# Two attention layers with expert layers between: token numbers in tile order, earlier splitting of h, and expert weights split three experts ahead

## The reference

```python
x = x + xattn0(layernorm(x), ctx)     # queries, keys and values from x, 1024 context rows per batch, plus 512 new ones
x = x + ffn0(layernorm(x))            # 8 experts, top 2, inner width 256: silu(x wi0) * (x wi1) wo
x = x + xattn1(layernorm(x), ctx)     # readout of the 1024 masked context rows, no projections
x = x + ffn1(layernorm(x))            # 32 experts, top 8, inner width 192
# x: (2, 512, 512) float32, so 1024 tokens = 8 tiles of 128
```

## Time and profile before

| | us |
|---|---|
| median of 3 runs | 1081.93 (1081.78 to 1082.22) |
| profiled execution, its own time | 1074.04 |
| its span | 1072.3 |
| TensorE busy in the span | 800.4 (75%) |
| GpSimd, ScalarE, VectorE busy | 476.3, 517.8, 517.3 |

### The profile page before, as it was taken

The page is one execution under the profiler, slowest core; times in us unless marked ns, Lnnn a source line. Parts: engine busy times, 40 slices in busy tenths (PEclk is TensorE's granted clock), DMA queues, the critical chain, the costliest instruction groups (busy, mean ns, idle before and its releaser), DMA issues.

```text
span 1072.3 us, 20533 instructions
## 1 busy us (share of the span) xinstructions
PE 800.4 (75%) x5262; PEld 438.2 (41%) x5263; DVE 517.3 (48%) x1531; ACT 517.8 (48%) x764; POOL 476.3 (44%) x397
## 2 busy tenths in 40 slices
PE   3999999999538995477984177777777778777770
PEld 2555455555324442233542043444444444444440
DVE  6344345555444552556884244544544535453432
ACT  2334234445436663135563065566656556655550
POOL 3420000001235774300777555666766566656560
PEclk9999999999769998697996599999999999999995
DMA  8501100000147876901111358878997878779668
GB/s 278 177 20 60 60 31 22 29 31 31 31 130 206 210 174 104 321 2 50 47 47 33 94 134 217 217 156 203 220 233 195 227 168 197 182 186 230 150 111 255
DMA packets 106088, 146.55 MB, mean 137 GB/s; under 512 B 18080, under 2 KB 59296, under 8 KB 106048
## 3 DMA queue, kind: packets, MB, share of 16 engines
q0 software_dynamic: 25760, 56.56, 26.6%
q1 hardware_dynamic: 77696, 89.30, 25.6%
q10 hardware_dynamic: 2592, 0.19, 0.2%
HBM read 103.15 MB, written 42.86 MB: 136 GB/s over the span
## 4 chain that ended last, share of the span: by engine, by line
PE 38%; DMA 18%; issue 11%; DVE 11%; DVEq 8%; ACT 5%; SPq 4%; POOL 3%; ACTq 2%; POOLq 0%
PE pst L181 31%; DMA big<-in_L_ffn_w_down_dram 8%; DMA x_rows<-mid,small 6%; DVEq L1100 3%; DMA mid<-moe_normalised_rows,small 3%; DVEq L1094 2%; PE pst L1204 2%; PE pst L453 2%; POOL moe_tokens_of_experts L934 2%; DMA big<-x_rows 1%; DVE big L1086 1%; DVE xn L284 1%; ACT big L1068 1%; DVE stats L272 1%; PE pst L893 1%
## 5 line engine op out<-in xcount | busy, mean ns | idle before, releaser
L181 PE MATMUL pst<-big,mid 128*128 (+1 forms) x1392 | 278.1, 351 | 28.7 <-DVE mid L1315 16.6
L934 POOL DMA_INDIRECT moe_tokens_of_experts<-token_no,small x80 | 83.7, 1046 | 307.0 <-DVE small L987 286.9
L1398 POOL DMA_INDIRECT x_rows<-mid,small x100 | 161.1, 1611 | 130.2 <-ACT mid L1259 66.4
L181 PEld LDWEIGHTS pst<-big,mid 128*128 128x128 f16 x1392 | 134.6, 100 | 137.7 <-issue 43.8
L1388 POOL DMA_INDIRECT mid<-moe_normalised_rows,small x106 | 113.9, 1075 | 90.3 <-DVE small L1305 29.3
L1204 PE MATMUL pst<-big,mid 128*128 x520 | 129.8, 382 | 1.4 <-ACT mid L1251 0.9
L1240 ACT ACTIVATE mid<-pst 128x1024 f16<-128x1024 f16 x102 | 103.8, 1017 | 54.2 <-PE pst L1176 47.2
L1176 PE MATMUL pst<-id,mid 128*128 128x128 f16 x816 | 64.8, 224 | 59.6 <-DMA mid<-moe_normalised_rows,small 54.2
L1315 DVE SCALAR_TENSOR_TENSOR mid<-pst,small,mid 128x192 f32<-128x192 f32 (+1 forms) x100 | 42.6, 426 | 118.4 <-ACT mid L1246 117.6
L181 PE MATMUL pst<-ctxN,mid 128*128 128x512 f16 x384 | 89.8, 392 | 3.2 <-ACT mid L577 3.2
L1176 PEld LDWEIGHTS pst<-id,mid 128*128 128x128 f16 x816 | 51.6, 100 | 94.4 <-DMA mid<-moe_normalised_rows,small 40.4
(11 more groups left out here) (197 smaller groups left out, 1163.0 us busy)
## 6 DMA issues: line engine op xcount, KB each, us to landing
big<-in_L_ffn_w_gate_dram SPq DMA_DIRECT2D x32, 384.0 KB
big<-in_L_ffn_w_up_dram SPq DMA_DIRECT2D x32, 384.0 KB
big<-in_L_ffn_wi_dram SPq DMA_DIRECT2D x16, 512.0 KB
big<-in_L_ffn_w_down_dram SPq DMA_DIRECT2D x32, 256.0 KB
big<-in_L_ffn_w_down_dram SPq DMA_DIRECT2D x64, 128.0 KB
moe_normalised_rows<-xn SPq DMA_DIRECT2D x18, 256.0 KB, 2.0
mid<-in_ctx_dram SPq DMA_DIRECT2D x16, 256.0 KB, 5.1
x_rows<-big SPq DMA_DIRECT2D x16, 256.0 KB, 8.0
```

The lines of the kernel that those rows point to most:

```text
L181: last = nc.tensor.matmul(dst, stationary(a, c), moving(b, c), start=(k == 0), stop=(k == 3 * len(parts) - 1))
L934: nc.gpsimd.indirect_dma_start(out=self.tab_d[:, :], out_offset=bass.IndirectOffsetOnAxis(ap=self.addr[j % 2][:, k:k + 1], axis=0), in_=to ...
L1398: nc.gpsimd.indirect_dma_start(out=acc_d[p][:, :], out_offset=bass.IndirectOffsetOnAxis(ap=self.si[p], axis=0), in_=self.y[p], in_offset=N ...
```

## The change

- **Token table.** The table in DRAM is laid out expert by expert and tile by tile, 128 numbers per row, so that the numbers of one tile of an expert are one row. SyncE's load of the table is gone. Instead `dve_route` works out the row `tidx` of each tile, GpSimd gathers those rows with one indirect DMA (`table_rows`), and `dve_rows` turns them with one TensorE transpose into `rows`, in which column t+2 holds the numbers of tile t. No column has to be loaded into a register.
- **VectorE's pair.** h of tile t is made and split at once, then come the row numbers for gather t+4 and the weights of t+2, then a split, then the row numbers for scatter t-1. Registers: 2 experts (`etab`) and 3 of `stab`.
- **Splits of weights.** `stab` holds the expert plus 3. ScalarE, GpSimd and VectorE all split expert e+3 in the slot after e's first tile, all in the same slot. `ftab` and its wait are gone.
- **Second expert layer.** Experts 0 to 3 are split within attn1 (ScalarE after iterations 1 to 4; all low halves on GpSimd, two experts before the first listing, one after each of the first two listings). Experts 4 and 5 are loaded meanwhile. In exp0 experts 2 and 3 are split in slots 0 and 1 whatever the tiles are.
- **Order in attention.** `logits` is issued between the two halves of `values`, `choose` and `place` move, GpSimd stores the spare accumulator rows after the first listing, not at the end. Routing semaphores are shared by both layers.

```diff
@@ three / values: the values product in two halves
-        def three(pe, dst, parts, stationary, moving):
+        def three(pe, dst, parts, stationary, moving, first=True, final=True):
...
+                three(pe, dst, range(half), lambda h, k: pT[:, h, k, :], val, final=False)
+                between()
+                three(pe, dst, range(half, n), lambda h, k: pT[:, h, k, :], val, first=False).then_inc(self.pv_full, 1)
@@ Attention.pe
-                    self.values(pe, i)
-                    if self.first and i >= 2:
-                        self.next.logits(pe, i - 2)
-                    if not self.first and i >= 1:
-                        self.next.logits(pe, i - 1)
+                    def between():
+                        if self.first and i >= 2:
+                            self.next.logits(pe, i - 2)
+                        if self.first and i == NT - 1:
+                            self.next.norm_turn(pe, NT - 2, self.norm_bank(NT - 2))
+                        if not self.first and i >= 1:
+                            self.next.logits(pe, i - 1)
+                    self.values(pe, i, between)
@@ Attention.act
+                    if not self.first and 1 <= i <= 4:
+                        self.next.split_early_hi(act, i - 1)
@@ Attention.dve, end of an iteration, and the tail
+                    if i >= (2 if self.first else 1):
+                        self.next.choose(dve, i - (2 if self.first else 1))
...
                 self.update(dve, NT - 1)
                 self.next.norm_row(dve, NT - 1)
-                self.next.choose(dve, NT - 2)
-                self.next.norm_low(dve, NT - 1)
                 self.next.weight(dve, NT - 3)
                 self.next.place(dve, NT - 2)
+                self.next.norm_low(dve, NT - 1)
+                self.next.choose(dve, NT - 1)
+                self.next.place(dve, NT - 1)
                 self.next.weight(dve, NT - 2)
-                self.next.choose(dve, NT - 1)
                 self.next.weight(dve, NT - 1)
-                self.next.place(dve, NT - 1)
@@ Experts
+            AHEAD = 3
...
+                    if not self.late and j in (1, 2, 4, 5):
+                        e = {1: 2, 2: 3, 4: 4, 5: 5}[j]
+                        self.load_next(sp, e, e % 2)
...
-            def table_sp(self, sp):
...
+            def table_rows(self, pool):
+                pool.wait_ge(self.tab_s, 3)
+                for q in range(2):
+                    pool.wait_ge(self.listed[q], 16 * NT // 2 * self.K)
+                nc.gpsimd.indirect_dma_start(out=self.trow, out_offset=None, in_=self.tiles_d[:, :],
+                                             in_offset=bass.IndirectOffsetOnAxis(ap=self.tidx, axis=0)).then_inc(self.trow_in, 16)
...
+            def split_early_hi(self, act, e):
+                if e == 0:
+                    act.wait_ge(back_s, NT)
+                self.split_hi(act, e)
+
+            def split_early_lo(self, pool, e):
+                pool.wait_ge(self.w_hi, 2 * e + 2)
+                nc.gpsimd.tensor_tensor(self.gu[:, e, 1, :, :], self.gur[:, e % 2, :, :], self.gu[:, e, 0, :, :], ALU.subtract).then_inc(self.wgu_lo, 1)
+                nc.gpsimd.tensor_tensor(self.d[:, e, 1, :, :], self.dr[:, e % 2, :, :], self.d[:, e, 0, :, :], ALU.subtract).then_inc(self.wd_lo, 1)
...
+            def dve_rows(self, dve):
+                NE = self.NE
+                dve.wait_ge(self.trow_in, 16)
+                nc.vector.tensor_copy(self.trow32, self.trow).then_inc(self.rows32_s, 1)
+                dve.wait_ge(self.route_pe, 4)
+                link(dve, nc.vector.tensor_copy(self.rows, bank(4)[:, 256:256 + NE]))
@@ act_pair
-                    if not first:
+                    if first:
+                        if self.late:
+                            self.split_hi(act, 2 + p)
+                    else:
                         self.weigh(act, it - 1, t - 2, p)
-                    with act.If(e[p + 1] > e[p]):
-                        self.split_hi(act, e[p + 1], self.first_tile(act, e[p + 1]))
+                        with act.If(e[p + 1] > e[p]):
+                            self.split_hi(act, e[p + 1])
@@ dve_pair
-                e = self.experts(dve, it, 0, 3)
-                c = self.columns(dve, it, -2, 7)
+                e = self.experts(dve, it, 2, 2)
+                x = None if first else self.splits(dve, it)
                 for p in range(2):
                     t = 2 * it + p
-                    self.rows_in_turn(dve, it + 1 + p, t + 3, 1 - p, c[5 + p])
-                    self.weights_in_turn(dve, it + 1 + p, t + 1, 1 - p, e[1 + p])
+                    self.make_h(dve, t, p)
+                    self.h_high(dve, t, p)
+                    self.h_low(dve, t, p)
+                    self.rows_in_turn(dve, it + 2, t + 4, p)
+                    self.weights_in_turn(dve, it + 2, t + 2, p, e[p])
+                    if first:
+                        if self.late:
+                            self.split_d_lo(dve, 2 + p)
+                    else:
+                        with dve.If(x[p + 1] > x[p]):
+                            self.split_d_lo(dve, x[p + 1])
                     if not (first and p == 0):
-                        self.h_high(dve, t - 1, 1 - p)
-                        self.h_low(dve, t - 1, 1 - p)
-                    with dve.If(e[p + 1] > e[p]):
-                        self.split_d_lo(dve, e[p + 1])
-                    self.make_h(dve, t, p)
-                    if not first:
-                        self.rows_out(dve, it - 1, t - 2, p, c[p])
+                        self.rows_out(dve, it - 1 + p, t - 1, 1 - p)
@@ pool_pair
-                e = self.experts(pool, it, 1, 3)
+                e = None if first else self.splits(pool, it)
                 for p in range(2):
                     t = 2 * it + p
                     self.gather(pool, t + 3, 1 - p)
-                    with pool.If(e[p + 1] > e[p]):
-                        self.split_gu_lo(pool, e[p + 1])
-                    if not first:
+                    if first:
+                        if self.late:
+                            self.split_gu_lo(pool, 2 + p)
+                    else:
+                        with pool.If(e[p + 1] > e[p]):
+                            self.split_gu_lo(pool, e[p + 1])
                         self.scatter(pool, it - 1, t - 2, p)
@@ GpSimd's program
+            exp1.split_early_lo(pool, 0)
+            exp1.split_early_lo(pool, 1)
             for j in range(NT):
                 exp1.list_tokens(pool, j)
-            pool.wait_ge(attn1.x_s, NT)
+                if j < 2:
+                    exp1.split_early_lo(pool, 2 + j)
+                if j == 0:
+                    exp1.spare_rows(pool)
             exp1.pool(pool)
```

383 lines of the change are left out of this document (194 added, 189 removed).

## The result

The changed kernel takes **1178.11 us** (median of 4 runs, 1172.60 to 1184.53) where the kernel before takes 1082.08 us (1081.78 to 1087.98): the ratio is 1.087, with a 95% interval of 1.083 to 1.091. It is 8.7% slower. The forecast said slower, but with 1100 us, a range of 1086 to 1116 us, and 1132 us for the dearest rival.

What follows compares the result with a forecast made beforehand. It took VectorE's late low half of h as today's wait and the three-slot gather chain as the next bound. Terms -1 (exp1), +4 (exp0), +15 (early splits), 0 made +18: 1074.0 to 1092, plus 7.9 for the median: 1100 us, range 1086 to 1116.

Steps and rivals of the forecast that it cites:

- a listing block of 8 takes 10.7 us: In attn1, GpSimd lists a block of 8 in 10.7 us, an iteration takes 12, so its queue has little room.
- each before the listing needs its addresses: In attn1, VectorE is held at place(4) to place(7), yet in time for the listing; attn1's own end isn't the bound.
- exp1, "-1 us": Second expert stage: 421 us against 422, from 72 slots at 5.36 us and 8 at 4.40, between 352 and 447.
- This part gives what the gather leaves: down to 4.40 us a slot: Splitting h at once in exp1's loop: three slots at least 13.2 us, one 4.40, 0.88 below today's, 70 us in 80 tiles.
- 2.7 us late: In exp1's loop, splits in one slot send the next gather 6.3 us after the down product's end instead of 3.6.
- exp0, "+4": First expert stage: 4 us gained, splits in the loop cost 7, two unconditional splits 1: +4 us, from -9 to +10.
- Early splits, "+15": Weight splits in attn1 delay the last listing by 15 us, 10 to 18: 8.5 + 10.9 + 1.2 - 5.6.
- "0 us" from the last listing to the first gather: Between attn1's last listing and exp1's first gather: 8.4 to 9.7 us against 8.6 before, so no change.
- The marks: In exp1: last listing near 615, first product 631, scatter 3.7 us behind y's copy, low-half waits under 10, gathers above 60.
- Splits fall into slack: Rival, chance 0.27: the loop's split delays cost little, exp1 374 us instead of 422, exp0 -5, listing +15: 1044 us.
- The scatter's buffer binds: Rival, chance 0.15: scatters landing before y may be rewritten set the slot; exp1 447 us, exp0 +8, listing +15: 1130 us.
- The listing's delay does not show: Rival, chance 0.08: attn1's early splits do not delay the path, since casts come sooner or blocks shrink: +3, 1085 us.

Runs made afterwards that it cites:

- e1: Kernel before, with token numbers written to side-by-side words as in the change and the table read back word by word: ratio 1.084.
- e17: Changed kernel, unchanged, profiled in the same series as the unchanged kernel before: span 1158.4 us, one run.
- e18: Changed kernel with exp1's token numbers 32 bytes apart and low halves subtracted a slot after the cast, early splits kept: 1069.96 us, ratio 1.000 in the medians.
- e4: Changed kernel with GpSimd and VectorE subtracting low halves one slot after ScalarE's cast in both expert loops: 1110.58 us, ratio 1.017.
- e2: Changed kernel with the second expert stage's token numbers 32 bytes apart in memory instead of 4: 1152.27 us, ratio 1.061.
- e13: Changed kernel with low halves a slot after the cast, exp1's weights loaded and split late, and its token numbers 32 bytes apart: 1078.03 us, ratio 0.992.
- e7: e4 with VectorE's copy of the scatter's row numbers one tile later: ratio 1.101.
- e8: Changed kernel with GpSimd issuing the scatter before the low-half subtraction, cast and subtraction still in one slot: 1118.98 us, ratio 1.030.
- e5: Kernel before, with both halves of h made right behind make_h in h's own slot: ratio 1.053.
- e14: e10 plus four pairs of unused GpSimd subtractions in attn1 at the early splits' places, without casts or loads: ratio 1.019.
- e10: Changed kernel with the scatter ahead of the subtraction, exp1's weights loaded and split late, and its token numbers 32 bytes apart: 1079.8 us, ratio 1.008.
- e16: Kernel before, unchanged, profiled again in the same series as the unchanged changed kernel: span 1066.8 us, one run.
- e9: Kernel before, with GpSimd issuing a slot's scatter ahead of the low-half subtraction: ratio 1.030.
- e12: Kernel before, with 32 semaphore increments nobody waits for at the start of ScalarE's, TensorE's and VectorE's programs: ratio 1.000.
- e11: e10 with the low halves also subtracted a slot after the cast: ratio 1.021.

## Why the prediction was wrong

The sign was right. On one chip the change costs 91.6 us where the sum has 18. Of the 73.6 us between them 31 lie in the middle, where a cause of 12 to 32 us was missing, and 32 in exp1, where the gain was put at 70 us and is 22; exp0 has 6 and the start 4.

**The missing cause.** The step that failed is "a listing block of 8 takes 10.7 us", with the half-sentence on VectorE at place(4) to place(7), "each before the listing needs its addresses". The forecast looked at the new addresses only for what the table load costs, and took the landing "as before". The words side by side hold the packets of queue q1, SyncE's, which brings weights and stores rows (78 to 204 ns in e1), and listings land after 5.6 us instead of 2.2 (e1, exp0). Shown by e1, by e17 against e18 (+31.6 us) and by e4 against e2 (+12.1 us). The start of exp0 (+4.4 us) has the same mark: in the profile after ScalarE's store of the router's weights took 8.78 us before exp0. That this is the addresses too was not tried, since every run with them has them in exp0.

**exp1, "-1 us".** Measured +31.3 on one chip, +34.8 between the profiles. The sum had two terms: a slot of 4.40 us if nothing delays the gather, and 69 us (72 slots from 4.40 to 5.36) for the splits in one slot. The second was a little too large: e17 against e18 gives 454.4 - 401.0 = 53.4 us in exp1 and 11.5 us in exp0. The first failed, and it is the step that failed in exp1. Without those delays a slot is 401.0/80 = 5.01 us (e18) or 5.09 us (e13), not 4.40: the change's other parts gain 22 us of exp1, not 70, and some 6 of these by the splits taken out. "This part gives what the gather leaves: down to 4.40 us a slot" treats the three-slot chain through the gather as the only bound. e7 and e8 show the other, through the scatter, and e5 that h at once is no gain where it is put ahead of the copies that release scatter and gather. I also charged the delay to the gather ("2.7 us late"); in e8 the gather keeps it and the scatter doesn't, and nearly all the time comes back. The sum also kept TensorE's work as it was, 4.02 us a slot; of exp1's +31.3 us 17.5 are that work at a lower clock. What binds the slot at 5.0 us once the scatter goes on time was not shown; TensorE then still waits 45.1 us for gathers, VectorE 71.9 us for scatters (e4).

The flights were not the fault, though they were misread. The medians of the earlier trace rows for the gather, 4.3 us, are over exp0's, the only ones whose landing that profile has, and they count from the start of the instruction, so the 1 us that I added is in them. In exp1 the median is 4.9 us from the start (e17, e18), where the sum took 5.8, and 5.0 to 5.2 us for a scatter, where it took 6.6.

**exp0, "+4".** +13.7 between the profiles, +9.9 on one chip: alignment +11.5, the rest -1.6, against 7 and some -4 and +1.

**Early splits, "+15".** 14.1 us in the middle, 16.4 on the last listing (10 to 11 us in series 1 against 2 and 4): right in size, though part of it comes by another way, GpSimd's subtractions stopping VectorE (4.6 us of path in e14), which the forecast had only as VectorE slowing GpSimd.

**"0 us" from the last listing to the first gather.** 17.3 us in the profile after and 14.6 in e17, where before it is 8.6: the last listing's landing, 11.73 us in the chain above. With 32 bytes it is 9.3 us in e10 and e18, within the 8.4 to 9.7 forecast, and 10.0 us in e2, but 13.1 us in e13 and e14, for which no run gives a reason.

**The marks.** The scatter stood 3.6 us behind ScalarE's copy, as forecast (3.7). Waits for gathers rose above 60 (88.5), also in e17 (77.0). Waits for the low half fell to 19.5, not under 10. The last listing ended at 665.9, not 615, the first product came at 689.2, not 631.

**The rivals.** "Splits fall into slack" is wrong. "The scatter's buffer binds" came nearest: +25 us in exp1 and +8 in exp0, against +31.3 and +9.9 on one chip, and e4, e7 and e8 show its mechanism, though 17.5 of the 31.3 us are slower products; its 1130 us lacks what the middle had. "The listing's delay does not show" is wrong. The 7.9 us between the profiled execution and the median were added in full; medians differ by 96.0 us, the two profiles by 107.1, e16 and e17 by 91.6, so the profiled pair overstates by what series differ in.

## What to carry to other kernels

When a change gives small writes new addresses, price what they do to everybody else's packets: look at the share of time of the queue that carries them, divided by its packets, and at the landing of the small ones, after a look at which of them have a landing in the trace. In a software pipeline with read-modify-write scatters, find the ring of every buffer, the scatter's as well as the gather's, before believing that one chain bounds the slot; then put work that may wait into the time in which a queue stands for the scatter's input, and nothing that can wait for another engine ahead of the scatter. Look also at what VectorE does while GpSimd subtracts. A step made "sooner" costs if it is put ahead of a copy that releases a transfer.

## What the runs showed of the hardware

Writes of 4 bytes to neighbouring words made packets of queue q1 2.6 to 3 times as long (78 to 204 ns in e1, 61 to 184 ns in e17 against e18), and landed themselves after 5.6 us instead of 2.2 (e1, exp0). 32 bytes apart they did neither (78 ns and 2.1 us in e10). While GpSimd subtracts, VectorE's operations of 0.19 us took 2.05 and 3.00 us, up to its end (after), and one of 0.23 us took 2.59 us (e9); with the subtraction behind the scatter in GpSimd's queue VectorE was busy 38 to 42 us more in exp1 (e8 against e4, e9 against e12, e11 against e13). TensorE's mean granted clock in exp1 was 0.96 before and 0.90 after the change (e16, e17), between its levels of 1.2 and 2.4 GHz, while it stood idle for 93.7 and 107.5 us; the same 2,232 products were 17.5 us longer in busy time. And one program differed by 16.9 us on one chip between two series. By the profiles of other kernels with the same attn1, 17 us of that size lie between its first and last listing; the cause stays open.
